# Rotary attention: the row sums of the denominators move from the vector engine to the scalar engine's accumulator output

## The chip, the cores and the metric

The kernel runs on one core of one Trainium2 chip. The metric is the device time of one execution in microseconds (us). TensorE is called PE in the profile, VectorE is DVE, ScalarE is ACT, GpSimd is POOL and SyncE, whose queue issues most DMAs, is SP.

## The reference

A two-layer network on x of shape (4, 1024, 128): plain attention, an FFN with rounded (FP4) operands, rotary attention, and a mixture of experts. The change is in the rotary attention alone, with 16 heads of 8 columns:

```python
attn_num = jnp.exp(jnp.einsum('bhqd,bhkd->bhqk', q_rot, k_rot) / scale)
attn_den = jnp.exp(jnp.einsum('bhqd,bhkd->bhqk', q, k) / scale)
attn_den = jnp.sum(attn_den, axis=-1, keepdims=True)
attn = attn_num / attn_den
causal = jnp.tril(jnp.ones((c, c), jnp.float32))[None, None]
attn = jnp.where(causal == 0, 0.0, attn)
y = jnp.einsum('bhqk,bhkd->bhqd', attn, v)
```

Numerator and denominator are different exponentials. The numerator is of the rotated q and k and is causal. The denominator is of the unrotated ones, over all 1024 keys, and of it only the sum of each row is wanted.

## The kernel before

The program is a chain of blocks: load, project, plain attention (`softmax_phase`), FFN, project with rotation, rotary attention (`causal_phase`), merge (`merge1_phase`), routing, experts. Between two blocks all engines meet at a barrier. The order inside a block is written out by hand: each engine has its own list of instructions, and semaphores join the lists.

`causal_phase` takes the 64 pairs of batch and head as G = 16 groups of HG = 4 heads. The work of a group is a list `seq` of U = 50 units, the same in each group. A unit fills two PSUM banks `cpsS` (128 partitions x 1024 columns) on PE, and one ACT instruction takes their exponential. There are three such pairs of banks, used in turn, so that the scores of unit n wait (`s_e`) for the exponential of unit n-3. The kinds of unit are:

- "wide" (16 in a group) and "lone" (2): numerators. Their exponentials go to `cprobs`. Later PE multiplies them with the values into `cpsO` (`chunk_sum`, L1010), ten times in a group, at places given by `sums`. One such step stands in PE's list behind the scores of its place.
- "den" (32 in a group, NDEN; 512 in all): denominators, 128 query rows against 1024 keys of one head. The exponential (L1044) goes to one of EX = 2 tiles `exps`. DVE then reads its two halves, adds them and sums the row (L1070) into one column of `den`. DVE counts this in `s_ds`, and the den exponential two dens later waits for it, since it writes the same `exps` tile.

The units stand as wide, den, den, wide, den, den, and so on, with a single den here and there. Besides L1070, DVE only copies finished sums out of `cpsO` (L1060, 32 times). `merge1_phase` begins with the reciprocal of `den` on DVE (L1385).

Of the kernel before, what the change touches and what calls it, by code (L numbers as in the profile page):

```python
# [7 lines left out]
BF16 = mybir.dt.bfloat16  # L8
I32 = mybir.dt.int32
U32 = mybir.dt.uint32  # L10
ALU = mybir.AluOpType
ACT = mybir.ActivationFunctionType
# [4 lines left out]
P = 128  # L17
TOK = B * N
T = TOK // P
TB = N // P  # L20
CH = 512
NCH = TOK // CH
TC = CH // P
HG = 4
# [6 lines left out]
SCALE = float(DH) ** -0.5  # L31
# [863 lines left out]
NDEN = HG * TB  # L895
# [28 lines left out]
def causal_phase(p, O, den, stacks):  # L924
# [4 lines left out]
    U = len(seq)  # L929
    place = {s: i for i, s in enumerate(seq)}  # L930
    done = {x: i + 1 for i, (_, x) in enumerate(sorted(sums.items()))}
    SUMS = len(done)
    EX = 2
    LOAD, v, s_ld = stacks.LOAD, stacks.v, stacks.s_ld
    with ExitStack() as c:
        def sb(name, shape, dt=F32):
            return c.enter_context(nc.sbuf_tensor(name, shape, dt))

        def sem(name):
            return c.enter_context(nc.semaphore(name))  # L940
        pr = [sb(f"cprobs{i}", [P, HG, 2, CH]) for i in range(2)]
        ex = [sb(f"exps{i}", [P, 2, CH]) for i in range(EX)]
        psS = [c.enter_context(nc.psum_tensor(f"cpsS{i}", [P, 2, CH], F32)) for i in range(3)]
        psO = [c.enter_context(nc.psum_tensor(f"cpsO{i}", [P, CH], F32)) for i in range(2)]
        s_ds = sem("exps_summed")
        s_s, s_e = sem("cscores_made"), sem("cexps_done")
        s_av, s_ev = sem("chunks_summed"), sem("csums_kept")
        s_oz = sem("psO_cleared")
# [3 lines left out]
        def _(pe):  # L952

            def part_of(g, cq, j, h, out, last):

                a = first_column(cq, j)
                _, _, kr, qr = (s[g % 2] for s in (stacks.stacks[0], stacks.stacks[1], stacks.stacks[3], stacks.stacks[2]))
                diagonal = j >= TC * cq
                ins = pe.matmul(out, kr[:, h, j * P:(j + 1) * P], qr[:, h, cq * CH + a:(cq + 1) * CH],  # L959
                                start=True, stop=not diagonal, skip_group_check=True)  # L960
                if diagonal:

                    ins = pe.matmul(out[:, 0:P], p.identb[:, :], p.maskb[:, :], start=False, stop=True,  # L963
                                    skip_group_check=True)
                return ins
# [24 lines left out]
            def chunk_sum(g, kind, x, chunk):  # L990
                n = g * SUMS + done[kind, x, chunk]
                if kind == "wide":
                    cq, halves = WIDE[x]
                    parts = halves[chunk]
                    made = place[kind, x, HG - 1]
                else:
                    cq, parts, made = x, [(TC * x + 2, 0)], place[kind, x, 0]

                pe.wait_ge(s_e, g * U + made + 1)
                if (kind, x, chunk) == ("wide", 0, 0):  # L1000

                    pe.wait_ge(stacks.s_v, g + 1)
                if chunk == 0 and kind == "wide" and x < 2 and g:

                    pe.wait_ge(s_ev, (g - 1) * 2 + cq + 1)
                for j, col in parts:
                    a = first_column(cq, j)
                    for h in range(HG):
                        rhs = pr[QUAD_ORDER.index((kind, x)) % 2][:, h, chunk, col:col + CH - a]
                        ins = pe.matmul(psO[cq][VW * h:VW * h + VH, a:CH], v[g % 2][:, j, h, :], rhs,  # L1010
                                        start=(j == 0), stop=(kind == "lone"), skip_group_check=True)
                ins.then_inc(s_av, 1)
# [14 lines left out]
        @block.scalar  # L1027
        def _(act):

            for g in range(G):  # L1030
                for u, (kind, x, y) in enumerate(seq):
                    n = g * U + u
                    if kind != "den":
                        quad = QUAD_ORDER.index((kind, x))
                        earlier, other = QUAD_ORDER[quad - 2], g if quad >= 2 else g - 1
                        if y == 0 and other >= 0:

                            act.wait_ge(s_av, other * SUMS + done[earlier[0], earlier[1], 1 if earlier[0] == "wide" else 0])
                    if kind == "den" and g * NDEN + x * TB + y >= EX:

                        act.wait_ge(s_ds, g * NDEN + x * TB + y - EX + 1)
                    act.wait_ge(s_s, n + 1)
                    if kind == "den":
                        act.activation(ex[y % EX][:, :, :], psS[n % 3][:, :, :], ACT.Exp, scale=SCALE).then_inc(s_e, 1)  # L1044
                    elif kind == "wide":
                        act.activation(pr[quad % 2][:, y, :, :], psS[n % 3][:, :, :], ACT.Exp, scale=SCALE).then_inc(s_e, 1)  # L1046
                    else:
                        act.activation(pr[quad % 2][:, :, 0, 0:LONE],
                                       psS[n % 3][:, :, :].rearrange("p b (h n) -> p (b h) n", n=LONE), ACT.Exp,
                                       scale=SCALE).then_inc(s_e, 1)  # L1050

        @block.vector
        def _(dve):
            for i in range(2):
                dve.memset(psO[i][:, :], 0.0).then_inc(s_oz, 1)  # L1055

            def keep(g, cq):

                dve.wait_ge(s_av, g * SUMS + done["lone", cq, 0])
                dve.tensor_copy(O[:, g, cq * CH:(cq + 1) * CH], psO[cq][:, :]).then_inc(s_ev, 1)  # L1060

            after = {max(u for u, x in sums.items() if x == ("lone", cq, 0)) + 1: cq for cq in range(2)}
            for g in range(G):
                for u, (kind, x, y) in enumerate(seq):
                    if kind == "den":

                        dve.wait_ge(s_e, g * U + u + 1)
                        at = g * NDEN + y * HG + x
                        two = ex[y % EX]
                        dve.tensor_tensor_reduce(two[:, 0, :], two[:, 0, :], two[:, 1, :], 1.0, 0.0, ALU.add, ALU.add,  # L1070
                                                 den[:, at:at + 1]).then_inc(s_ds, 1)
                    if g and u + U in after:
                        keep(g - 1, after[u + U])
                    if u in after:
                        keep(g, after[u])
            keep(G - 1, 1)

        @block.gpsimd
        def _(pool):
            for g in range(2, G):  # L1080

                pool.wait_ge(s_av, (g - 1) * SUMS)
                stacks.fill(pool, g % 2, g)
# [720 lines left out]
def build(nc, ins, outs):  # L1804
    (z, w_qkv0, w_gate, w_up, w_down, w_qkv1, w_out, b_out, router, w1, w2, bias, cos, sin) = ins
    with ExitStack() as ctx:
        p = Program(nc, ctx)
        with ExitStack() as c0:
            values = c0.enter_context(nc.sbuf_tensor("values", [P, G, TB, HG * DH], F32))
            stacks = Rotary(p, c0, values)  # L1810
            with ExitStack() as cw:
                fw = FfnWeights(p, cw)
                load_phase(p, z, fw, w_gate, w_up, w_down)
                with ExitStack() as c:
                    plain = Plain(p, c, values)
                    project_phase(p, w_qkv0, None, plain, fw)
                    softmax_phase(p, plain, stacks, fw)
                ffn_phase(p, fw)
            project_phase(p, w_qkv1, (cos, sin), stacks)
            with ExitStack() as c:  # L1820
                O = c.enter_context(nc.sbuf_tensor("sums1", [P, G, N], F32))
                den = c.enter_context(nc.sbuf_tensor("den", [P, G * HG * TB], F32))
                causal_phase(p, O, den, stacks)
                merge1_phase(p, O, den, w_out, b_out)
        with ExitStack() as c:
            xn = c.enter_context(nc.sbuf_tensor("tokens_normed", [P, T, ROW], F32))
            slots = c.enter_context(nc.sbuf_tensor("slots", [P, 2, T], U32))
            s_sent = [c.enter_context(nc.semaphore(f"tokens_sent{k}")) for k in range(2)]
            route_phase(p, xn, slots, s_sent, router)
            expert_phase(p, xn, slots, s_sent, w1, w2, bias, outs[0])  # L1830
# [30 lines left out]
```

## Time and profile before

| what | value |
|---|---|
| time, median of 3 runs | 2166.07 us (2159.33 to 2167.11) |
| the profiled execution's own time | 2166.85 us |
| its span, first to last instruction | 2165.0 us |
| mean granted TensorE clock | 0.925 |
| PE, DVE, ACT busy over the span | 1708.6, 1395.3, 1481.7 us |
| DMA | 113.83 MB, mean 53 GB/s |

The span is what the rows of the trace add up to; 1.85 us of the profiled execution lie outside it. `causal_phase` runs from about 1107 to 1853 us of the span. Busy shares over the whole span average blocks with different limits, so the block around the change is read by itself.

### The profile page before, as it was taken

What the parts mean: (1) busy time and instruction counts of PE and PEld (TensorE: products, weight loads), DVE (VectorE), ACT (ScalarE), POOL (GpSimd) and SP (SyncE); (2) the same over time, 40 slices, a digit from 0 to 9 for tenths busy, and PEclk for the clock granted to TensorE, in tenths of its full rate; (3) what the DMA queues carried; (4) which work ended last, traced back from release to release, by engine and by line L of the source; (5) the groups of instructions that cost most, each with busy time, mean ns of one, the idle gap of its engine ahead of it and who ended that gap; (6) DMA issues with size and microseconds to landing.
All of it is one profiled execution on the core that took longest, in us unless ns stands there. A gap on an engine that the chain in (4) does not pass through costs nothing. (4 is left out here: it accounts for less than half of the span.)

```text
span 2165.0 us, 33156 instructions
## 1 busy us (share of the span) xinstructions
PE 1708.6 (79%) x12896; PEld 647.6 (30%) x12968; DVE 1395.3 (64%) x2570; ACT 1481.7 (68%) x2167; POOL 285.8 (13%) x272
## 2 busy tenths in 40 slices
PE   5399999999999995665768888888888888741695
PEld 3022222222222222443322222222222222540474
DVE  7799999999999946996655555555555555561112
ACT  4168778777877784332479999999999999310121
POOL 4300000000000001432320000000000000017554
PEclk9589999999999997897889999999999999955797
DMA  4200000010000001003431111111111110005133
GB/s 140 92 5 36 31 24 24 29 37 28 24 24 30 21 2 78 0 0 133 164 124 48 45 48 56 57 56 49 44 49 57 55 56 6 3 12 163 51 100 104
DMA packets 70093, 113.83 MB, mean 53 GB/s; under 512 B 7298, under 2 KB 56392, under 8 KB 64304
## 3 DMA queue, kind: packets, MB, share of 16 engines
q1 hardware_dynamic: 64688, 94.96, 12.3%
q0 software_dynamic: 5248, 16.75, 2.0%
q8 instruction: 102, 1.67, 0.3%
q14 instruction: 55, 0.45, 0.1%
HBM read 73.58 MB, written 37.95 MB: 52 GB/s over the span
## 5 line engine op out<-in xcount | busy, mean ns | idle before, releaser
L786 ACT ACTIVATE probs<-psS 128x512 f32<-128x512 f32 x1024 | 556.5, 596 | 187.9 <-PE psS L690 186.4
L805 DVE TENSOR_REDUCE max_of_halves<-psM 128x2 f32<-128x1024 f32 x512 | 617.8, 1222 | 46.6 <-PE psM L659 17.1
L1070 DVE CUSTOM_DVE_ANT_0 exps<-exps 128x512 f32<-128x512 f32 x512 | 354.6, 693 | 367.2 <-ACT exps L1044 367.2
L1044 ACT ACTIVATE exps<-cpsS 128x1024 f32<-128x1024 f32 x512 | 526.2, 1116 | 0.0
L976 PE MATMUL cpsS<-rotary_stack 128*128 128x512 bf16 x976 | 287.5, 384 | 82.3 <-ACT exps L1044 73.0
L710 PE MATMUL psO<-probs,plain_v 128*9 128x256 f32 x4096 | 317.2, 382 | 4.9 <-issue 2.2
L1046 ACT ACTIVATE cprobs<-cpsS 128x1024 f32<-128x1024 f32 x256 | 286.5, 1119 | 5.7 <-PE cpsO L1010 3.5
L659 PE MATMUL psM<-plain_top 64*128 64x512 bf16 x1024 | 212.3, 395 | 39.8 <-DVE max_of_halves L805 22.7
L959 PE MATMUL cpsS<-rotary_stack 128*128 128x512 bf16 (+3 forms) x744 | 188.3, 328 | 52.9 <-ACT cprobs L1046 51.6
L690 PE MATMUL psS<-plain_top 64*128 64x512 bf16 x1024 | 213.4, 388 | 7.4 <-issue 6.1
L690 PE MATMUL psS<-plain_rest 64*128 64x512 bf16 x1024 | 207.7, 377 | 0.0
L976 PEld LDWEIGHTS cpsS<-rotary_stack 128*128 128x128 bf16 x1024 | 64.9, 97 | 303.4 <-ACT exps L1044 274.5
L1010 PE MATMUL cpsO<-cprobs,rotary_v 128*9 128x512 f32 (+3 forms) x1536 | 153.7, 488 | 0.0
L1763 ACT ACTIVATE e_ht<-e_psH 128x1024 f32<-128x1024 f32 x32 | 32.8, 1024 | 140.1 <-PE e_psH L1732 67.1
L959 PEld LDWEIGHTS cpsS<-rotary_stack 128*128 128x128 bf16 x768 | 67.2, 98 | 203.4 <-ACT cprobs L1046 148.4
L710 PEld LDWEIGHTS psO<-probs,plain_v 128*9 128x9 f32 x4096 | 61.3, 88 | 220.7 <-issue 120.1
L690 PEld LDWEIGHTS psS<-plain_top 64*128 64x128 bf16 x1024 | 59.6, 93 | 223.4 <-ACT probs L786 191.3
L963 PE MATMUL cpsS<-maskb,identb 128*128 128x128 bf16 x512 | 93.5, 220 | 12.3 <-DVE cpsO L1055 10.7
L465 POOL COPY plain_v<-values 128x256 f32<-128x256 f32 x16 | 6.4, 402 | 655.4 <-PE psO L710 655.4
L465 POOL COPY rotary_v<-values 128x256 f32<-128x256 f32 x16 | 6.4, 403 | 650.2 <-PE cpsO L1010 650.2
L659 PEld LDWEIGHTS psM<-plain_top 64*128 64x128 bf16 x1024 | 58.2, 95 | 113.3 <-DVE max_of_halves L805 48.3
L301 PE MATMUL p_psQ<-p_xt,p_w 128*128 128x512 f32 x96 | 61.7, 749 | 25.4 <-DVE p_rest L400 25.2
(210 smaller groups left out, 1757.3 us busy)
## 6 DMA issues: line engine op xcount, KB each, us to landing
rotary_stack<-q_parts SPq DMA_DIRECT2D x48, 192.0 KB
rotary_stack<-k_parts SPq DMA_DIRECT2D x48, 192.0 KB
rotary_stack<-q_rot_parts SPq DMA_DIRECT2D x48, 192.0 KB
rotary_stack<-k_rot_parts SPq DMA_DIRECT2D x48, 192.0 KB
q_parts<-p_part SPq DMA_DIRECT2D x16, 384.0 KB, 4.4
k_parts<-p_part SPq DMA_DIRECT2D x16, 384.0 KB, 3.6
plain_top<-q_parts SPq DMA_DIRECT2D x64, 96.0 KB
plain_top<-k_parts SPq DMA_DIRECT2D x64, 96.0 KB
```

Of the source, the lines that this page charges most:

```text
L659: ins = pe.matmul(psM[n % 2][:, e, :], tq[g % 3][rows, hh, t * P:(t + 1) * P], tk[g % 3][rows, hh, kh * CH:(kh + 1) * CH], start=True, sto ...
L690: ins = pe.matmul(psS[u % RING][:, :], k[rows, hh, j * P:(j + 1) * P], q[rows, hh, cq * CH:(cq + 1) * CH], start=(part == 0), stop=(part = ...
L710: ins = pe.matmul(psO[VW * h:VW * h + VH, columns], v[g % 2][:, j, h, :], pr[n % SLOTS_P][:, h, columns], start=(j == 0 and part == 0), st ...
L786: act.activation(pr[n % SLOTS_P][:, h, :], psS[u % RING][:, :], ACT.Exp, scale=SCALE).then_inc(s_e, 1)
L805: dve.tensor_reduce(mh[g % 2][:, :, hh, t, kh:kh + 1].rearrange("p e o -> p (e o)"), psM[n % 2][:, :, :], AX.X, ALU.max).then_inc(s_r, 1)
L959: ins = pe.matmul(out, kr[:, h, j * P:(j + 1) * P], qr[:, h, cq * CH + a:(cq + 1) * CH], start=True, stop=not diagonal, skip_group_check=True)
L963: ins = pe.matmul(out[:, 0:P], p.identb[:, :], p.maskb[:, :], start=False, stop=True, skip_group_check=True)
L976: ins = pe.matmul(to[:, kh, :], q[:, x, y * P:(y + 1) * P], k[:, x, kh * CH:(kh + 1) * CH], start=True, stop=True)
L1010: ins = pe.matmul(psO[cq][VW * h:VW * h + VH, a:CH], v[g % 2][:, j, h, :], rhs, start=(j == 0), stop=(kind == "lone"), skip_group_check=True)
L1044: act.activation(ex[y % EX][:, :, :], psS[n % 3][:, :, :], ACT.Exp, scale=SCALE).then_inc(s_e, 1)
L1046: act.activation(pr[quad % 2][:, y, :, :], psS[n % 3][:, :, :], ACT.Exp, scale=SCALE).then_inc(s_e, 1)
L1070: dve.tensor_tensor_reduce(two[:, 0, :], two[:, 0, :], two[:, 1, :], 1.0, 0.0, ALU.add, ALU.add, den[:, at:at + 1]).then_inc(s_ds, 1)
```

## The change

A den exponential now gives its row sum itself: the ACTIVATE has an accumulator output, `accum_out`, which is the column of `den`. The DVE instruction L1070 and the semaphore `exps_summed` are gone. Nobody reads the tiles `exps` any more, and they become bf16. Two writes to the same `exps` tile are now kept apart by ACT's own semaphore: a den waits until `s_e` counts the exponential two dens before.

```diff
+    made = [place["den", d // TB, d % TB] for d in range(NDEN)]
     EX = 2
...
-        ex = [sb(f"exps{i}", [P, 2, CH]) for i in range(EX)]
+        ex = [sb(f"exps{i}", [P, 2, CH], BF16) for i in range(EX)]
...
-        s_ds = sem("exps_summed")
...
-                    if kind == "den" and g * NDEN + x * TB + y >= EX:
-
-                        act.wait_ge(s_ds, g * NDEN + x * TB + y - EX + 1)
                     act.wait_ge(s_s, n + 1)
                     if kind == "den":
-                        act.activation(ex[y % EX][:, :, :], psS[n % 3][:, :, :], ACT.Exp, scale=SCALE).then_inc(s_e, 1)
+                        at = g * NDEN + y * HG + x
+                        if g * NDEN + x * TB + y >= EX:
+
+                            act.wait_ge(s_e, made[(x * TB + y - EX) % NDEN] + (g if x * TB + y >= EX else g - 1) * U + 1)
+                        act.activation(ex[y % EX][:, :, :], psS[n % 3][:, :, :], ACT.Exp, scale=SCALE,
+                                       accum_out=den[:, at:at + 1]).then_inc(s_e, 1)
...
-                    if kind == "den":
-
-                        dve.wait_ge(s_e, g * U + u + 1)
-                        at = g * NDEN + y * HG + x
-                        two = ex[y % EX]
-                        dve.tensor_tensor_reduce(two[:, 0, :], two[:, 0, :], two[:, 1, :], 1.0, 0.0, ALU.add, ALU.add,
-                                                 den[:, at:at + 1]).then_inc(s_ds, 1)
```

On ACT, early in the first group, the program held this before (`cprobs` are numerators, `exps` denominators; the semaphores waited for stand in brackets):

```order
L1044 ACTIVATE exps<-cpsS 128x1024 [waits cscores_made,exps_summed]
L1046 ACTIVATE cprobs<-cpsS 128x1024 [waits cscores_made]
L1044 ACTIVATE exps<-cpsS 128x1024 [waits cscores_made,exps_summed] x2
L1046 ACTIVATE cprobs<-cpsS 128x1024 [waits cscores_made]
L1044 ACTIVATE exps<-cpsS 128x1024 [waits cscores_made,exps_summed] x2
L1048 ACTIVATE cprobs<-cpsS 128x4x256 [waits cscores_made]
L1044 ACTIVATE exps<-cpsS 128x1024 [waits cscores_made,exps_summed]
L1046 ACTIVATE cprobs<-cpsS 128x1024 [waits cscores_made,chunks_summed]
```

And at the same place it holds this now:

```order
L1045 ACTIVATE exps,den<-cpsS 128x1024 [waits cexps_done,cscores_made]
L1048 ACTIVATE cprobs<-cpsS 128x1024 [waits cscores_made]
L1045 ACTIVATE exps,den<-cpsS 128x1024 [waits cexps_done,cscores_made] x2
L1048 ACTIVATE cprobs<-cpsS 128x1024 [waits cscores_made]
L1045 ACTIVATE exps,den<-cpsS 128x1024 [waits cexps_done,cscores_made] x2
L1050 ACTIVATE cprobs<-cpsS 128x4x256 [waits cscores_made]
L1045 ACTIVATE exps,den<-cpsS 128x1024 [waits cexps_done,cscores_made]
L1048 ACTIVATE cprobs<-cpsS 128x1024 [waits cscores_made,chunks_summed]
```

The order of the exponentials is the same, and each den has as many waits as before. In the compiled program each of the 512 rows that write `exps,den` is two ScalarE instructions: the ACTIVATE, and behind it one that reads the accumulator and writes the column of `den`. The completion count `cexps_done` (`s_e`) stands at the second.

On DVE, within the groups, the program held this before (the two ISA rows are the sum and the read of DVE's own accumulator, `sums` is where `cpsO` is copied to):

```order
L1070 ISA exps,den<-exps 128x512 [waits cexps_done]
L1070 ISA den 128x1
L1060 COPY sums<-cpsO 128x512 [waits chunks_summed]
L1070 ISA exps,den<-exps 128x512 [waits cexps_done]
L1070 ISA den 128x1
```

Now DVE's whole list in `causal_phase`, and the start of the merge behind it, is this:

```order
L1057 MEMSET cpsO 128x512 x2
L1062 COPY sums<-cpsO 128x512 [waits chunks_summed] x32
...
L1380 RECIPROCAL m_rden<-den 128x512
L1382 TENSOR_TENSOR X<-X,m_bias 128x4096 [waits bias_loaded]
L1399 TENSOR_TENSOR m_y<-m_psO,m_rden 128x128 [waits sums_turned,dve_start]
```

All 1024 ISA rows are gone, and the 32 copies follow one another. PE's list keeps its order.

## Rows read from the trace of the kernel before

**Rows 1.** The page: granted clock and busy tenths, 40 slices of 54 us.

```profile
DVE  7799999999999946996655555555555555561112
ACT  4168778777877784332479999999999999310121
...
PEclk9589999999999997897889999999999999955797
```

**Rows 2.** Busy time of the engines in stretches of the rotary attention.

```profile
core 0: us, PE busy (x) PEld busy (x) DVE busy (x) ACT busy (x) POOL busy (x), PEclk, DMA share, GB/s
...
1200.00:1400.00 200.00, 163.67 (x1038) 49.80 (x1060) 101.93 (x285) 198.95 (x216) 2.01 (x5) 1.00 0.13 53
1400.00:1700.00 300.00, 243.82 (x1506) 71.70 (x1526) 152.84 (x427) 297.98 (x325) 2.42 (x6) 1.00 0.13 53
```

**Rows 3.** Costliest groups: busy us, mean ns; idle time before, and its releaser.

```profile
L1070 DVE CUSTOM_DVE_ANT_0 exps<-exps 128x512 f32<-128x512 f32 x512 | 354.6, 693 | 367.2 <-ACT exps L1044 367.2
L1044 ACT ACTIVATE exps<-cpsS 128x1024 f32<-128x1024 f32 x512 | 526.2, 1116 | 0.0
```

**Rows 4.** Waits from 1110 to 1855 us: total us, times, longest.

```profile
ACT cprobs L1046 <- PE cpsO L1010: 3.5, 16, 0.2
ACT cprobs L1046 <- PE cpsS L963: 1.7, 2, 1.4
```

**Rows 5.** Lines L1044, L1046: duration ns min/median/max, first and last start.

```profile
L1044 ACT ACTIVATE exps<-cpsS x512: 1017/1099/1282, 1110.8 to 1851.0; 128x1024 f32<-128x1024 f32 x171
...
L1046 ACT ACTIVATE cprobs<-cpsS x256: 1024/1092/1293, 1109.9 to 1846.5; 128x1024 f32<-128x1024 f32 x128
```

**Rows 6.** Timeline from 1402 us: start, duration, idle before.

```profile
1401.30 1.93 ACT L1044 ACTIVATE exps<-cpsS 128x1024 f32<-128x1024 f32 x2
...
1402.97 0.08 DVE L1070 DVE_READ_ACCUMULATOR2_ANT den<- 128x1 f32 x1
1403.11 1.04 ACT L1046 ACTIVATE cprobs<-cpsS 128x1024 f32<-128x1024 f32 x1
1403.27 0.69 DVE L1070 CUSTOM_DVE_ANT_0 exps<-exps 128x512 f32<-128x512 f32 x1 [0.22 <-ACT exps L1044]
...
1403.29 0.60 PE L976 MATMUL cpsS<-rotary_stack 128*128 128x512 bf16 x2 [0.31 <-ACT exps L1044]
1403.88 0.08 DVE L1070 DVE_READ_ACCUMULATOR2_ANT den<- 128x1 f32 x1
1403.88 0.69 DVE L1060 COPY sums<-cpsO 128x512 f32<-128x512 f32 x1
```

**Rows 7.** Timeline from 1396 us, around a pause of ACT.

```profile
1395.39 1.11 ACT L1046 ACTIVATE cprobs<-cpsS 128x1024 f32<-128x1024 f32 x1
...
1396.30 2.04 ACT L1044 ACTIVATE exps<-cpsS 128x1024 f32<-128x1024 f32 x2
...
1396.55 0.28 PE L959 MATMUL cpsS<-rotary_stack 128*128 128x256 bf16 x1 [0.31 <-ACT cprobs L1046]
...
1398.11 1.15 ACT L1048 ACTIVATE cprobs<-cpsS 128x1024 f32<-128x1024 f32 x1
...
1399.01 1.16 ACT L1044 ACTIVATE exps<-cpsS 128x1024 f32<-128x1024 f32 x1
...
1399.26 1.05 PE L1010 MATMUL cpsO<-cprobs,rotary_v 128*9 128x384 f32 x16
...
1400.38 1.02 ACT L1046 ACTIVATE cprobs<-cpsS 128x1024 f32<-128x1024 f32 x1 [0.22 <-PE cpsO L1010]
```

**Rows 8.** Timeline of ACT alone from 1004 us: short ACTIVATEs of a project block.

```profile
1004.41 0.22 ACT L330 ACTIVATE p_w<-p_psQ 128x64 f32<-128x64 f32 x1
1004.51 0.23 ACT L331 ACTIVATE p_w<-p_psQ 128x64 f32<-128x64 f32 x1
1004.62 0.30 ACT L326 ACTIVATE p_w<-p_psQ 128x128 f32<-128x128 f32 x1
1004.77 0.26 ACT L330 ACTIVATE p_w<-p_psQ 128x64 f32<-128x64 f32 x1
```

**Rows 9.** Timeline at the end of the rotary attention.

```profile
1850.12 2.04 ACT L1044 ACTIVATE exps<-cpsS 128x1024 f32<-128x1024 f32 x2
...
1850.33 1.48 PE L1010 MATMUL cpsO<-cprobs,rotary_v 128*9 128x384 f32 x24
...
1852.81 0.69 DVE L1060 COPY sums<-cpsO 128x512 f32<-128x512 f32 x1
```

## The prediction, made before the changed kernel ran

> **What bounds the kernel now.** I read the page's slices first. In the slices of the rotary attention, from about 1110 to 1853 us, ACT shows 9 throughout, DVE 5 and the granted clock 9, its full mark [rows 1]. The stretches say it more sharply: of 200 us ACT is busy 198.95, and of 300 us 297.98, so 99.4%. PE is busy 82% and DVE 51%, at clock 1.00 [rows 2]. So ACT bounds this block, a third of the span.
>
> Next come the groups by line. The DVE sum L1070 is 512 x 693 ns = 354.6 us of work, and DVE sat idle 367.2 us before it, waiting for the exponentials. Before L1044, the exponential of the dens, ACT's idle time is 0.0 [rows 3]. In the list of waits, ACT waits for PE alone, 5.2 us in all, and never for DVE [rows 4]. The wait on `s_ds` that the change removes is therefore worth nothing.
>
> What ACT needs for one unit isn't its duration of 1116 ns, since an ACTIVATE starts before the one ahead has ended. Their starts give the price: 1401.30 to 1403.11 for two, thus 0.905 us each [rows 6], and again 1396.30 to 1398.11 [rows 7]. For 16 x 50 = 800 units that makes 724 us. The first starts at 1109.9 and the last at 1851.0 [rows 5], so with the last one's own 0.905 they take 742 us, and 18 us are pauses. One is seen whole: 1399.01 to 1400.38 is 1.37 us, 0.465 above 0.905, and its end waits for PE's `cpsO` [rows 7].
>
> **The change part by part.**
>
> *DVE's work goes* (512 sums and accumulator reads). Nobody on the path waits for DVE inside the block, so this gives 0 there. At the block's end it gives a little. The last copy starts at 1852.81, behind two sums, while PE's last product ends at 1850.33 + 1.48 = 1851.81. The last exponential ends at about 1850.12 + 2.04 = 1852.16 [rows 9]. Today the copy ends at 1853.50. Then the block would end by the last accumulator read or by the copy, at about 1852.7. **-0.8 us.**
>
> *The exponential itself* keeps its 1024 columns. That adding up on the way makes a column no dearer is my assumption. No row before has an ACTIVATE with an accumulator output; from below it costs 0, and a rise in price per column is left to the range.
>
> *512 accumulator reads come onto ACT, the engine that bounds the block.* This is the term that decides, and no row shows it on ACT. I bound it by the nearest rows:
> - From below: nothing. DVE has the same pair of instructions. Its read takes 0.08 us by itself, but the copy behind it starts in the same instant, 1403.88, and the read starts 0.61 us after a sum that lasts 0.69 [rows 6]. There the read fits into the tail of its sum and costs the queue nothing.
> - In the middle: a slot of its own, like a very short ACTIVATE. Those of 64 columns start 0.10 and 0.11 us apart, and behind one of 128 columns the next starts 0.15 later [rows 8]. From 64 columns at 0.105 to 1024 at 0.905 it is 0.800 us for 960 columns, so 0.833 ns each. What is left at zero columns is 0.105 - 0.053 = 0.052 us. A read writes one column: 0.053 us. 512 x 0.053 = **27.1 us**. If there is a smallest slot, the 0.105 of 64 columns bounds it: 53.8 us.
> - From above: the read starts only when its ACTIVATE has ended. The shortest den takes 1.017 us [rows 5], which is 0.112 after the 0.905. With 0.053 for the read that is 0.165 a den, 84.5 us. If the next ACTIVATE also waits the read out, the read counts whole, as a 64-column ACTIVATE (0.22) without its columns (0.053), 0.167: 0.279 a den, 142.8 us.
>
> I take the middle, because ACT's rows at three lengths lie on one line, while the DVE row is of another engine.
>
> The Trainium skill (ScalarE: Activation LUTs, section What ACT_TABLE_LOAD costs) gives an ACTIVATE 186 ns + 0.833 ns a column and lets neighbours overlap by about 93 ns. By its figures the fixed part would be an estimated 93 ns where the rows give 52, the 512 reads 48 us, and the time 2208. On the price of a column the trace agrees, with 0.833.
>
> *The pauses give part of it back.* A pause ends when a chain on PE ends. In the one shown, PE starts the chain when the wide exponential of 1395.39 has ended and works until the products of 1399.26 are done. In that time ACT passes three dens (two at 1396.30, one at 1399.01) [rows 7]. Their reads push ACT's own next start 3 x 0.053 = 0.16 us later, while PE's chain stays where it is. So 0.16 of 0.465 us, a third, is absorbed. A third of 18 us is **-6 us**; 0 and -18 are the ends.
>
> *The count `s_e` moves to the read*, so that PE gets its bank later, by 0.05 to 0.17 us. In the flow this is hidden. PE's scores of 1403.29 are done at 1403.89, for an ACTIVATE that starts three places after the second of the two from 1401.30, at about 1404.9, thus with 1.0 us to spare [rows 6]. Without that cover the delay would stand in ACT's path whole, 512 x 0.05 = 26 us.
>
> *The new wait of ACT on itself.* A den waits for the exponential two dens before, three places or more back in ACT's list, 2.7 us ago by starts. The longest one takes 1.293 us [rows 5]. It is met each time: 0. Behind it, if it were late, stand all of ACT's later exponentials, and with them PE.
>
> *bf16 `exps`*: nobody reads them, and the write isn't what paces ACT, as far as rows show. 0, with a doubt taken up as a rival.
>
> **Sum**, against the profiled execution's own 2166.85 us (the median of the runs is 0.8 lower, so the two stand for the same time): 2166.85 + 27.1 - 6 - 0.8 = **2187 us**, 0.9% slower.
>
> **The rivals.**
>
> *A, the forecast, 0.45*: a read is a slot of 52 to 105 ns. From 27.1 with 12 of the pauses absorbed, 2181, to 53.8 with 10 absorbed, 2210.
>
> *B, the read is free, 0.20*: it slips into the tail of its ACTIVATE, as on DVE. For it speaks that DVE row. Against it, that ACT's fixed part is only 0.052 us, where DVE's 693 ns sum leaves 0.08 of tail in which the next may start. Time: 2166.85 - 0.8 = 2166, no change.
>
> *C, the read waits for the end, 0.30*: a sum isn't complete before the last column has gone through, and the rows show 0.112 us and more between the next possible start and the end of an ACTIVATE. Reads of 0.165 absorb all pauses: 2166.85 + 84.5 - 18 - 0.8 = 2233 (0.20). With the read counted whole: 2166.85 + 142.8 - 18 - 0.8 = 2291 (0.10). Against it: a read that goes through the same pipe behind the last column needs no wait.
>
> *D, it becomes faster, 0.05*: ACT's durations grow along a run without a pause (1.11 at 1395.39, 1.15 at 1398.11, 1.16 at 1399.01) [rows 7], up to 1.293 [rows 5]. The ends fall behind the starts. If the writing of 4 bytes a column holds the ends back, bf16 lets dens end up to 0.2 us earlier; PE gets its banks earlier, and the chains that end the pauses shorten. That gives at most the 18 us of pauses and needs a free read too. It passes the mark of 0.5% (10.8 us) only if 10 of the 18 us go: half of this case, at about 2155.
>
> That the change doesn't do what it says, I exclude: the DVE rows are gone from the program.
>
> **How the numbers follow.** 0.5% either way is about what a measurement of this kernel can tell from no change. The likeliest case gives 2187, by itself 2181 to 2210. The range takes in B and the first form of C with some 15 us for its error: 2160 to 2250. It leaves out C's second form (0.10), the faster end of D, and errors at the rims, together just under 0.2. Faster by over 0.5%: 0.04. Within 0.5% (up to 2177): B, and what of A and D falls there, 0.19. Slower: the rest, 0.77.
>
> **What would show it.** After the change ACT should have 512 more rows, of accumulator reads. The distance from a den's start to the next ACTIVATE should be 0.96 us in a run without a pause (A), 0.905 (B), 1.07 or 1.18 (C). ACT should stay over 99% busy there and the block should be some 20 us longer. The pause at the first wide unit after a lone one should shrink from 0.465 to 0.31 us. DVE should fall to the 32 copies, and the reciprocal of the merge should come about 0.8 us earlier behind the last exponential. All other blocks should be as long as before. The prediction is wrong if a den's distance is outside 0.93 to 1.02 us, if PE's scores come late because of the later count, or if a column costs more with the accumulator on.

## The result

The changed kernel takes 2198.76 us (median, 2196.3 to 2203.6) against 2164.14 us for the kernel before: a ratio of 1.0165, 95% interval 1.0137 to 1.0193. It is slower by 34.6 us. The forecast was 2187, with a range of 2160 to 2250, so the direction and the mechanism held. The size was off: 21 us were forecast against 34.6.

Of the changed kernel's page, the span and the busy tenths of the slices:

```profile
span 2198.7 us, 32644 instructions
DVE  7799999999999928996500000000000000361012
ACT  4167877778877883324489999999999999410121
PEclk9589999999999997888899999999999999955797
```

DVE's work in the rotary attention has gone from 5 to 0, ACT stays at 9, and the granted clock shows 9 throughout the block as before [rows 1]. The block has only become longer. Its groups on the page say what ACT does there:

```profile
L1045 ACT ACTIVATE exps<-cpsS 128x1024 bf16<-128x1024 f32 x512 | 567.9, 1192 | 0.0
L1062 DVE COPY sums<-cpsO 128x512 f32<-128x512 f32 x32 | 22.1, 692 | 758.6 <-PE cpsO L1010 758.6
...
L1045 ACT ACTIVATION_READ_ACCUMULATOR exps<-cpsS 128x1 f32 x512 | 193.6, 378 | 0.0
```

There are 512 new rows, as forecast. Their mean of 378 ns is not their price. An instruction can start before the one ahead has ended, so the price is the distance from its start to the next start. The timeline of ACT in the changed kernel gives that (start, duration):

```profile
1406.08 1.26 ACT L1048 ACTIVATE cprobs<-cpsS 128x1024 f32<-128x1024 f32 x1
1406.98 1.27 ACT L1045 ACTIVATE exps<-cpsS 128x1024 bf16<-128x1024 f32 x1
1407.88 0.45 ACT L1045 ACTIVATION_READ_ACCUMULATOR exps<-cpsS 128x1 f32 x1
1407.98 1.28 ACT L1045 ACTIVATE exps<-cpsS 128x1024 bf16<-128x1024 f32 x1
1408.88 0.46 ACT L1045 ACTIVATION_READ_ACCUMULATOR exps<-cpsS 128x1 f32 x1
1408.97 1.28 ACT L1048 ACTIVATE cprobs<-cpsS 128x1024 f32<-128x1024 f32 x1
```

A read starts 0.90 us after its den, as any next unit would. The instruction behind it starts 0.09 to 0.10 us after the read. To the nanosecond it is 0.0925 us on the mean of the 224 reads that stand between two dens. So 512 reads take 47.4 us of slots. They neither wait for the end of the den (rival C) nor come for nothing (rival B). From a den's start to the next unit's it is 0.997 us: above the 0.96 of the forecast, but within the 0.93 to 1.02 outside which it was to be called wrong.

The block as a whole is measured by the first start (L1048) and the last den's start (L1045):

```profile
L1045 ACT ACTIVATE exps<-cpsS x512: 1017/1213/1331, 1110.2 to 1887.0; 128x1024 bf16<-128x1024 f32 x171
...
L1048 ACT ACTIVATE cprobs<-cpsS x256: 1024/1187/1287, 1109.3 to 1882.2; 128x1024 f32<-128x1024 f32 x128
```

1887.0 - 1109.3 = 777.7 us, where before it was 1851.0 - 1109.9 = 741.1 [rows 5]: 36.6 us more. The span grew by less, 33.7 us, because the rest of the program became some 3 us shorter: 0.6 us ahead of the block, 1.0 at its end and 1.4 after it.

### The profile page after: what moved, and what is told of

It is laid out like the page before. It is cut to its first block and busy times, and to the rows that moved or that the text cites. A ratio compares the mean times of both kernels' runs of the same rounds, so it can differ in the third digit from the quotient of the medians.

```text
span 2198.7 us, 32644 instructions
## 1 busy us (share of the span) xinstructions
PE 1706.7 (78%) x12896; PEld 642.3 (29%) x12968; DVE 1040.4 (47%) x1546; ACT 1522.8 (69%) x2679; POOL 285.6 (13%) x272
## 5 line engine op out<-in xcount | busy, mean ns | idle before, releaser
L1045 ACT ACTIVATE exps<-cpsS 128x1024 bf16<-128x1024 f32 x512 | 567.9, 1192 | 0.0
L1062 DVE COPY sums<-cpsO 128x512 f32<-128x512 f32 x32 | 22.1, 692 | 758.6 <-PE cpsO L1010 758.6
L1048 ACT ACTIVATE cprobs<-cpsS 128x1024 f32<-128x1024 f32 x256 | 298.9, 1168 | 1.4 <-PE cpsS L963 1.4
L1045 ACT ACTIVATION_READ_ACCUMULATOR exps<-cpsS 128x1 f32 x512 | 193.6, 378 | 0.0
L1758 ACT ACTIVATE e_ht<-e_psH 128x1024 f32<-128x1024 f32 x32 | 32.8, 1024 | 139.0 <-PE e_psH L1727 102.1
```

## The experiments

Below, "the block" is the time from the first start of a numerator to the start of the last den, in `causal_phase`: 741.1 us before, 777.7 changed. Times without a ratio are one profiled execution's. The times of the kernel before differ by up to 9 us from execution to execution (2159.1 to 2167.8), so 1 or 2 us between two such spans say little. The block is the firmer measure.

**dve_gone** leaves the row sums out altogether; `den` is filled with ones.

```diff
-                        act.activation(ex[y % EX][:, :, :], psS[n % 3][:, :, :], ACT.Exp, scale=SCALE,
-                                       accum_out=den[:, at:at + 1]).then_inc(s_e, 1)
+                        act.activation(ex[y % EX][:, :, :], psS[n % 3][:, :, :], ACT.Exp, scale=SCALE).then_inc(s_e, 1)
...
+            dve.memset(den[:, :], 1.0)
```

> The changed kernel without the accumulator output: neither ACT nor DVE sums the rows, and den is filled with ones once, so the output is not the reference's. It holds all other parts of the change (no DVE sums, bf16 exps, ACT's wait on its own semaphore). Theory (the reads' slots are the whole loss): the time of before less 0.8 us, 2164 to 2166 us against 2166, ACT's starts 0.904 us apart, pauses of some 18 us in the block as before. Rival 1 (bf16 writes or the missing DVE let exponentials end earlier, so that pauses shrink): 3 to 10 us below before. Rival 2 (the new wait of ACT on itself costs): above before, up to the 34 us that the change cost.

Measured: 2164.57 against 2164.96 us, ratio 0.9999 (0.9989 to 1.0008).

```profile
L1045 ACT ACTIVATE exps<-cpsS x512: 1017/1093/1287, 1109.1 to 1848.5; 128x1024 bf16<-128x1024 f32 x171
...
L1047 ACT ACTIVATE cprobs<-cpsS x256: 1024/1080/1293, 1108.1 to 1844.0; 128x1024 f32<-128x1024 f32 x128
```

The block is 740.4 us, 0.7 under that of before. So DVE's 512 sums, `s_ds`, the bf16 tiles and ACT's wait on itself are worth nothing together. The whole loss comes with the accumulator output.

**both_sums** adds the accumulator output to the kernel before and keeps DVE's sums.

```diff
+        spare = sb("spare", [P, NDEN])
...
-                        act.activation(ex[y % EX][:, :, :], psS[n % 3][:, :, :], ACT.Exp, scale=SCALE).then_inc(s_e, 1)
+                        at = g * NDEN + y * HG + x
+                        act.activation(ex[y % EX][:, :, :], psS[n % 3][:, :, :], ACT.Exp, scale=SCALE,
+                                       accum_out=den[:, at:at + 1]).then_inc(s_e, 1)
...
-                                                 den[:, at:at + 1]).then_inc(s_ds, 1)
+                                                 spare[:, at % NDEN:at % NDEN + 1]).then_inc(s_ds, 1)
```

> The kernel before, with the accumulator output on ACT added (it gives den) and DVE's sums kept, into a tile that nobody reads. Theory (reads are the loss, DVE's work is worth nothing inside the block): as the changed kernel, span 2199 plus up to 1 us, a read's slot 0.093 us. Rival (DVE's reading of exps or its semaphore also costs once ACT is slower): 5 us or more above the changed kernel.

Measured: span 2200.6 us, block 777.7. The block is that of the changed kernel, with fp32 tiles and DVE at work. The span is 1.9 us longer, of which 1.2 stand at the block's end, where the last sums are again ahead of the merge; that is 1 us more than expected and far from the rival's 5. So the loss needs neither the bf16 tiles nor DVE's absence, and what DVE's absence gains is 1.2 us at the block's end.

**half_reads** lets ACT sum every second den and DVE the others.

```diff
+                                       accum_out=den[:, at:at + 1] if y % 2 else None).then_inc(s_e, 1)
...
+                        if y % 2:
+                            dve.engine_nop().then_inc(s_ds, 1)
+                            continue
```

> Of the 512 dens, the 256 with odd y are summed by ACT's accumulator, the others by DVE as before. Theory (0.093 us a read, pauses absorb part of it, first units first): 256 x 0.093 = 23.8 us of slots, of which 6 to 12 us are absorbed, span 2165 + 12 to 18 = 2177 to 2183. Rival (the accumulator mode costs something once, or its first reads are free): a span that is not about half way, under 2172 or over 2190.

Measured: span 2178.3 us, block 756.5. 256 reads are 23.7 us of slots, of which 15.4 arrive and 8.3 are absorbed. The cost goes by the reads, and the first ones find the pauses.

**all_reads** gives the wide numerators an accumulator output too.

```diff
-                        act.activation(pr[quad % 2][:, y, :, :], psS[n % 3][:, :, :], ACT.Exp, scale=SCALE).then_inc(s_e, 1)
+                        act.activation(pr[quad % 2][:, y, :, :], psS[n % 3][:, :, :], ACT.Exp, scale=SCALE,
+                                       accum_out=spare[:, 4 * x + y:4 * x + y + 1]).then_inc(s_e, 1)
```

> The changed kernel with the accumulator output on its 256 wide numerators too (into a spare tile), so 768 reads. Theory (a slot of 0.093 us each, the reads first eat the 8 us of pauses that the changed kernel still has): 256 x 0.093 = 23.7 us more slots, 2 to 8 us of them absorbed, span 2198.7 + 16 to 22 = 2215 to 2220. Rival (what the change cost is not in proportion to the reads): under 2208 or over 2225.

Measured: span 2222.4 us, block 801.0. The 256 further reads (23.7 us of slots) add 23.3 to the block. The cost is in proportion, but the span missed the 2215 to 2220 that I expected: I had the reads absorb 2 to 8 us of what looked like pauses, and they absorbed 0.4. So after 512 reads hardly a real pause is left.

**tiny_activate** asks whether the read is special. It puts an ACTIVATE of one column behind each den of the kernel before, and the completion count `s_e` stays at the den.

```diff
+                        act.activation(spare[:, y:y + 1], p.ident[:, y:y + 1], ACT.Exp)
```

> The kernel before with one more ACTIVATE of one column (identity tile in, a spare tile out, no semaphore) behind each of the 512 den exponentials, and no accumulator output. Theory A (my step was wrong for every instruction: a one-column ACTIVATE has a slot of 0.093 us or more as well, since short ones have a floor): the next start 0.09 to 0.10 us after the tiny one, span 2195 to 2202. Theory B (the line through 64, 128 and 1024 columns holds to one column, and the accumulator read is dearer than a short ACTIVATE): 0.053 us, span about 2165 + 27 - 8 = 2184.

Measured: span 2201.5 us, block 777.3. The timeline of ACT in tiny_activate:

```profile
1403.29 1.24 ACT L1045 ACTIVATE exps<-cpsS 128x1024 f32<-128x1024 f32 x1
1404.19 0.42 ACT L1046 ACTIVATE spare<-ident 128x1 f32<-128x1 f32 x1
1404.29 1.24 ACT L1045 ACTIVATE exps<-cpsS 128x1024 f32<-128x1024 f32 x1
```

Again 0.09 to 0.10 us. The read is no dearer than an ACTIVATE of one column. It was my price of a short ACTIVATE that was wrong. Two explanations stay: a floor, the least that any instruction takes, or a fixed part that goes by where the input lies.

This run also shows what the count `s_e` costs at the read. Where PE waits for a den, its next scores start 0.056 us after the den's end here (0.055 in the kernel before), and 0.146 us after it in the changed kernel, on the median. So with the reads PE gets its bank 0.09 us later. Yet the block is 777.3 us here and 777.7 in both_sums, so this delay is worth at most 0.4 us.

**sizes** gives that ACTIVATE 4 to 64 columns, by the den's y.

```diff
+                        width, to = ((4, 0), (16, 4), (32, 20), (40, 52), (48, 92), (52, 140), (56, 192), (64, 248))[y]
+                        act.activation(spare[:, to:to + width], p.ident[:, 0:width], ACT.Exp)
```

> The kernel before with one more ACTIVATE behind each den exponential (identity tile in, a spare tile out), of 4, 16, 32, 40, 48, 52, 56 or 64 columns by the den's y. It asks why the line from 64, 128 and 1024 columns, 0.052 us + 0.833 ns a column, missed the 0.093 us of the one-column instruction. Theory F (a floor: an instruction's slot is the line, but at least 0.093 us): 0.093 for 4 to 48 columns, 0.095 for 52, 0.099 for 56, 0.105 for 64. Theory S (a fixed part of 0.093 us where the input isn't PSUM, as the three rows of the prediction all read PSUM): 0.096 for 4, 0.106 for 16, 0.126 for 40, 0.146 for 64.

Measured: span 2214.6 us. The timeline of ACT in sizes:

```profile
1405.87 1.41 ACT L1045 ACTIVATE exps<-cpsS 128x1024 f32<-128x1024 f32 x1
1406.77 0.65 ACT L1047 ACTIVATE spare<-ident 128x64 f32<-128x64 f32 x1
1406.93 1.41 ACT L1049 ACTIVATE cprobs<-cpsS 128x1024 f32<-128x1024 f32 x1
...
1410.65 0.62 ACT L1047 ACTIVATE spare<-ident 128x16 f32<-128x16 f32 x1
1410.76 1.43 ACT L1045 ACTIVATE exps<-cpsS 128x1024 f32<-128x1024 f32 x1
```

The medians of the distance to the next start, over some 64 of each, are 0.095 us for 4 columns, 0.105 for 16, 0.119 for 32, 0.132 for 48 and 0.146 for 64. These lie on 0.092 + 0.00083 a column. The floor falls, and theory S, a fixed part by the input, holds: with an input in SBUF it is 0.092, not 0.052.

**tiny_psum** is the counterpart: the one column comes from the PSUM bank. It is built on dve_gone, so it makes no sums either.

```diff
-                        act.activation(ex[y % EX][:, :, :], psS[n % 3][:, :, :], ACT.Exp, scale=SCALE).then_inc(s_e, 1)
+                        act.activation(ex[y % EX][:, :, :], psS[n % 3][:, :, :], ACT.Exp, scale=SCALE)
+                        act.activation(spare[:, y:y + 1], psS[n % 3][:, 1, y:y + 1], ACT.Exp, scale=SCALE).then_inc(s_e, 1)
```

> dve_gone (no sums at all, den filled with ones) with one more ACTIVATE of one column behind each den exponential, whose input is a column of the same PSUM banks; it carries the completion count, as the accumulator read does in the changed kernel. Theory (ACT's fixed part goes by the input: 0.052 us with an input in PSUM, 0.093 without): the next start 0.052 to 0.054 us after it, span 2161 + 27.1 less 6 to 10 us of absorbed pauses = 2178 to 2182. Rival (0.093 is the floor of any instruction that short, and the rows of 4 to 64 columns of the run sizes lie above it by chance of their SBUF input): 0.093 us, span 2197 to 2200.

Measured: span 2187.9 us. The timeline of ACT in tiny_psum:

```profile
1366.35 1.08 ACT L1046 ACTIVATE exps<-cpsS 128x1024 bf16<-128x1024 f32 x1
1367.25 0.24 ACT L1047 ACTIVATE spare<-cpsS 128x1 f32<-128x1 f32 x1
1367.30 1.11 ACT L1046 ACTIVATE exps<-cpsS 128x1024 bf16<-128x1024 f32 x1
...
1374.79 1.27 ACT L1046 ACTIVATE exps<-cpsS 128x1024 bf16<-128x1024 f32 x1
```

The next start comes 0.05 us later, as my line said for one column with its input in PSUM. The price by starts is confirmed, but the span isn't: 26.7 us over dve_gone's 2161.2 and nothing absorbed, where I had 17 to 21. The durations show why. From 1366.35 to 1374.79, nine units, they grow by 0.19 us; in the kernel before it is some 0.11 us in nine units. This is taken up below.

**lone_tile** and **lone_spread** look for what the pauses are, and for a kernel better than both. Both are the kernel before, DVE's sums kept. The first gives the lone numerators a tile of their own, beside the two `cprobs`, so that the exponential of a wide unit doesn't wait for a product just issued. The second also puts two products (`chunk_sum`) three units apart in PE's list in place of two.

```diff
+        lp = sb("clone", [P, HG, LONE])
-        ex = [sb(f"exps{i}", [P, 2, CH]) for i in range(EX)]
+        ex = [sb(f"exps{i}", [P, 2, CH], BF16) for i in range(EX)]
...
-                        rhs = pr[QUAD_ORDER.index((kind, x)) % 2][:, h, chunk, col:col + CH - a]
+                        rhs = pr[x % 2][:, h, chunk, col:col + CH - a] if kind == "wide" else lp[:, h, col:col + CH - a]
...
-                        earlier, other = QUAD_ORDER[quad - 2], g if quad >= 2 else g - 1
+                        earlier, other = (("wide", (x - 2) % 4), g if x >= 2 else g - 1) if kind == "wide" else (
+                            ("lone", 1 - x), g if x else g - 1)
...
-                        act.activation(pr[quad % 2][:, y, :, :], psS[n % 3][:, :, :], ACT.Exp, scale=SCALE).then_inc(s_e, 1)
+                        act.activation(pr[x % 2][:, y, :, :], psS[n % 3][:, :, :], ACT.Exp, scale=SCALE).then_inc(s_e, 1)
...
-                        act.activation(pr[quad % 2][:, :, 0, 0:LONE],
+                        act.activation(lp[:, :, :],
```

In lone_spread also:

```diff
-            free += 2
+            free += 3
```

> The kernel before, DVE sums kept, with a small tile of its own for the lone numerators, so that the wide ones alternate over the two cprobs tiles and no exponential waits for a product that has just been issued; exps are bf16 to make room for it. Theory (the pauses of 12 us in front of wide exponentials are waits for cpsO products; the 6 us in front of dens are late scores): the 12 us go, the 6 stay, span 2165 - 12 = 2153, ratio 0.994 to 0.996. Rival (PE's scores are behind anyway, so that the pause moves to the next unit): 2160 to 2166, ratio over 0.997.

> lone_tile, and the two products of a quad stand three units apart in PE's list in place of two, which gives PE's scores more room between them. Theory (the remaining 6 us of pauses come from two products too close together): another 4 to 6 us less, span 2147 to 2149, ratio 0.991 to 0.994. Rival (they come from one product, 1.0 us long, in front of scores): no change against lone_tile.

Measured: lone_tile 2160.56 us, ratio 0.9981 (0.9971 to 0.9990), block 736.0. The waits for `cpsO` are gone from ACT's list, but only 5 of the 12 us with them; smaller pauses appear at other units. That is the rival: its ratio was over 0.997. lone_spread takes 2156.98 us, ratio 0.9963 (0.9949 to 0.9977), block 732.4. The second step gives 3.6 us more, short of the 4 to 6 that I expected of it, and the ratio is above the 0.991 to 0.994 that I gave, since the first step had already fallen short. It still beats both kernels, and its interval is clear of 1: 8 us under the kernel before and some 42 under the changed one, which was not measured beside it.

**lone_reads** is the changed kernel with the lone tile.

> The changed kernel with the lone tile of lone_tile. Theory (the 10.8 us that the pauses absorbed were all that softened the 47.4 us of slots): with the reads absorbing the pauses of the lone_tile kernel too, the block's starts span 800 x 0.904 + 47.4 + 0 to 3 = 771 to 774 us, the whole span 2190 to 2195, 31 to 36 above lone_tile. Rival (PE's later release by the read's count becomes a wait once ACT pauses less): over 776 us.

Measured: span 2197.8 us, block 775.9. That is above the theory's 774, and its span is above the 2195; it is just under the rival's 776. So the theory missed, and the rival isn't shown. What it does show: taking away waits of ACT for PE, worth 5.1 us in the block without reads, is worth 1.8 with them.

## Why the prediction was right, and where it was not

*What bounds the block, and DVE's work worth 0.* Right. dve_gone measures no difference, and both_sums has the changed kernel's block with DVE at work.

*The exponential keeps its price with the accumulator on.* Right, though it was called an assumption. All 512 distances from a den to its read are 0.904 or 0.905 us.

*512 accumulator reads, 27.1 us.* The mechanism was right, a slot of its own each, but the size was off: 47.4 us. This term was mis-sized, by 20.3 us. I took the fixed part from rows that all read PSUM, where it is 0.052, and applied it to an instruction that has no PSUM input. sizes and tiny_psum separate the two. They differ in more than the input, though: the column of tiny_psum also has a scale and the count. The trace of before had the row I should have taken. ACT's timeline in its second project block alternates between an input in PSUM (`p_psQ`) and one in SBUF (`p_rest`), both of 512 columns, both a plain copy with a count:

```profile
1034.32 0.59 ACT L367 ACTIVATE p_part<-p_psQ 128x512 bf16<-128x512 f32 x1
1034.80 0.63 ACT L353 ACTIVATE p_part<-p_rest 128x512 bf16<-128x512 f32 x1
1035.32 0.60 ACT L367 ACTIVATE p_part<-p_psQ 128x512 bf16<-128x512 f32 x1
```

Behind the PSUM one the next starts after 0.48 us, behind the SBUF one after 0.52. Less 512 x 0.833 ns = 0.427, that is 0.05 and 0.09. So the place of the input is enough for the difference. Where the next one's input lies doesn't matter: between two with their inputs in SBUF, at 1090.40, it is 0.52 again.

```profile
1090.40 0.61 ACT L353 ACTIVATE p_part<-p_rest 128x512 bf16<-128x512 f32 x1
1090.92 0.62 ACT L367 ACTIVATE p_part<-p_rot 128x512 bf16<-128x512 f32 x1
```

That the read, which has no input tile, costs what an SBUF input costs is measured; that it does so for the same reason isn't shown. The estimate of 93 ns from the Trainium skill (ScalarE: Activation LUTs, section What ACT_TABLE_LOAD costs), which I had set aside for the rows, agrees with the read (0.0925), with tiny_activate (0.093) and with sizes (0.092). It doesn't agree with ACTIVATEs that read PSUM (0.051 in tiny_psum). Both prices lie within case A's bounds of 0.052 to 0.105, and so the time stayed in the range.

*The pauses give 6 us back.* By starts, as I had counted, 47.4 - 36.6 = 10.8 us were absorbed. Part of that is luck: it offsets a quarter of the reads' error of 20.3 us. The chain was read rightly and its pause was not. Here is that same pause in the changed kernel, with PE:

```profile
1408.97 1.28 ACT L1048 ACTIVATE cprobs<-cpsS 128x1024 f32<-128x1024 f32 x1
...
1410.31 0.28 PE L959 MATMUL cpsS<-rotary_stack 128*128 128x256 bf16 x1 [0.31 <-ACT cprobs L1048]
...
1412.78 1.32 ACT L1045 ACTIVATE exps<-cpsS 128x1024 bf16<-128x1024 f32 x1
...
1413.02 1.05 PE L1010 MATMUL cpsO<-cprobs,rotary_v 128*9 128x384 f32 x16
...
1414.14 1.02 ACT L1048 ACTIVATE cprobs<-cpsS 128x1024 f32<-128x1024 f32 x1
```

PE's chain starts when the wide exponential ends, at 1410.25, and ACT goes on at 1414.14, 3.89 us later. Before it was from 1396.50 to 1400.38, 3.88 [rows 7]. On the median of the 16 groups it is 3.885 before, 3.883 changed and 3.884 in tiny_activate, so the chain stays as it was, with the later count or without. All three reads are absorbed: from the end of the one wide exponential to the end of the other it is 4.909 us before and 4.908 changed. But from the den's start at 1412.78 to the wide one's at 1414.14 it is 1.36 us, of which 0.997 are the den and its read. That leaves 0.37 where 0.465 was and where I had forecast 0.31. The reason is in the wide exponential itself, which now lasts 1.28 us and not 1.11, so that the chain starts 0.17 later behind its start. Distances of starts thus show more of a pause than ACT has; the last section takes this up. At the other places they shrink too: at unit 39 of a group 1.195 became 0.904, at unit 37 0.984 became 0.904, and at the group's first 1.168 became 1.106, of which 0.093 is now a read.

*The end of the block, -0.8 us.* Right: -1.0. In the changed kernel the last den starts at 1887.04 and the reciprocal at 1889.21, 2.17 us later. Before it was 1854.16 behind 1851.02, 3.14.

```profile
1887.04 1.33 ACT L1045 ACTIVATE exps<-cpsS 128x1024 bf16<-128x1024 f32 x1
...
1889.21 3.35 DVE L1380 RECIPROCAL m_rden<-den 128x512 f32<-128x512 f32 x1 [0.67 <-PEq L936]
```

*The new wait on itself, and bf16, 0.* Right, by dve_gone. *The later count of `s_e`, 0.* Right within 0.4 us, by tiny_activate against both_sums. It isn't hidden everywhere, though. In all_reads the wide exponentials have reads too, so the chain above starts at a read, and the wide one's end is 3.974 us away in place of 3.884.

The sum with what was measured, term by term: 2166.85 + 47.4 - 10.8 - 1.0 - 1.9 (the rest of the program) = 2200.5, the changed kernel's profiled time of 2200.53. It closes because the absorbed part and the rest are themselves differences of measured times.

## What to carry to other kernels

An accumulator output on ScalarE isn't free where ScalarE is the bound: each is a second instruction with a slot of 0.09 us, and here the block became 5% longer. That it pays where ScalarE waits and the engine relieved doesn't is what one would expect, but no run here shows it. Before a fixed cost is taken from the nearest rows, look at where their inputs lie, and take a row that agrees in that. And before counting pauses as room to absorb new work, look at the distances between ends and not only between starts: the engine may not have been idle.

## What the runs showed that I had not expected

**Starts are not ACT's pace.** In a run without a pause the starts of the kernel before are 0.904 or 0.905 us apart, but durations grow, so the ends are further apart. Two of its rows, six units from each other:

```profile
1369.39 1.22 ACT L1046 ACTIVATE cprobs<-cpsS 128x1024 f32<-128x1024 f32 x1
...
1374.82 1.29 ACT L1046 ACTIVATE cprobs<-cpsS 128x1024 f32<-128x1024 f32 x1
```

The ends are at 1370.61 and 1376.11: 5.50 us for six, 0.917 each. In the changed kernel, twelve units and eight reads lie between these two:

```profile
1366.38 1.02 ACT L1045 ACTIVATE exps<-cpsS 128x1024 bf16<-128x1024 f32 x1
...
1377.97 1.12 ACT L1045 ACTIVATE exps<-cpsS 128x1024 bf16<-128x1024 f32 x1
```

Ends at 1367.40 and 1379.09, 11.69 us. Less 12 x 0.917 it is 0.69 for eight reads, 0.086 each. In tiny_psum nine units and six one-column ACTIVATEs take from 1367.43 to 1376.06; less 9 x 0.917 it is 0.38, 0.063 each. With these prices blocks come out nearly without a pause to explain them: 800 x 0.917 + 512 x 0.086 = 777.6 (measured 777.7), with 768 reads 799.6 (801.0), tiny_psum 765.9 (767.3), and without reads 733.6 (lone_spread 732.4).

All distances between the ends of neighbouring units say the same. In the kernel before the median is 0.917. In the changed one it is 0.914 without a read between them and 1.005 with one. What goes beyond the usual distance is real idleness: 9.0 us before, at 47 places, and not 18; 1.2 us in the changed kernel and 0.1 in lone_spread. So by ends the reads took the pauses nearly whole, some 8 us. This also fits two stretches of the changed kernel (the window and its length, then busy time with the count of instructions for PE, PEld, DVE, ACT and POOL, the granted clock, the DMA share and GB/s). ACT is busy for the whole of each:

```profile
1200.00:1400.00 200.00, 156.56 (x974) 45.89 (x996) 5.53 (x8) 200.00 (x338) 1.61 (x4) 1.00 0.12 48
1400.00:1700.00 300.00, 234.24 (x1463) 68.97 (x1484) 8.99 (x13) 300.00 (x506) 2.82 (x7) 1.00 0.12 50
```

It fits that all_reads, tiny_psum and lone_reads absorbed less than I expected, and it leaves lone_spread nothing more to gain from waits. What holds the ends back by 0.012 us a unit stays open; it isn't the fp32 write, since in dve_gone the ends of two dens in a row, written as bf16, are 0.917 us apart too. That the sum by ends accounts for the blocks is arithmetic on rows; no run was made to vary it alone.
